# Shared expert's weights split into halves by the Pool engine during the last attention

## What is computed

```python
x = x + xattn(layernorm(x), ctx)     # 16 heads of 32; rms-normed q and k; image and text softmax apart, then summed
x = x + ffn(layernorm(x))            # 32 experts, 4 of them per token, capacity 80, and a shared expert

def ffn_shared(x):                   # shared_gate, shared_up, shared_down: 512x512 each
    return silu(x @ shared_gate.T) * (x @ shared_up.T) @ shared_down.T
```

## Time and profile before

| | |
|---|---|
| median of 3 runs | 1188.79 us (1188.22 to 1189.98) |
| the profiled execution's own time | 1194.59 us |
| its span | 1192.8 us |
| PE busy | 1116.2 us, 94% |
| DVE busy | 856.9 us, 72% |
| ACT busy | 650.6 us, 55% |
| POOL busy | 202.1 us, 17% |

### The profile page before, as it was taken

One profiled execution on the slowest core, in us unless ns is written; L12 is line 12 of the kernel. 1 busy time (PEld: TensorE's weight loads), 2 busy tenths in 40 slices (PEclk: granted clock), 3 DMA queues, 4 the chain that ended last, 5 costly groups with the idle time before them and its releaser, 6 DMA issues. The chain is left out here.

```text
span 1192.8 us, 21823 instructions
## 1 busy us (share of the span) xinstructions
PE 1116.2 (94%) x8948; PEld 415.7 (35%) x8948; DVE 856.9 (72%) x1056; ACT 650.6 (55%) x916; POOL 202.1 (17%) x307
## 2 busy tenths in 40 slices
PE   7899999999999989999999999887999989999996
PEld 3342223344222334322233432222544433333332
DVE  6777889897898988788889879997789842222221
ACT  5559997444999644699955469883311121221121
POOL 1220000243000024300002430002100021333442
PEclk9999999999999999999999999999999999999999
DMA  8851000768200096900028780104813337999742
GB/s 299 199 109 43 2 2 10 194 135 201 54 2 2 20 228 136 203 8 2 2 72 194 171 215 31 36 3 136 359 60 109 113 113 285 348 317 313 215 62 33
DMA packets 142860, 150.15 MB, mean 126 GB/s; under 512 B 108833, under 2 KB 109089, under 8 KB 137761
## 3 DMA queue, kind: packets, MB, share of 16 engines
q1 hardware_dynamic: 135328, 131.57, 38.1%
q0 software_dynamic: 5120, 10.82, 4.9%
q10 hardware_dynamic: 2304, 6.29, 2.2%
HBM read 101.96 MB, written 21.51 MB: 104 GB/s over the span
## 5 line engine op out<-in xcount | busy, mean ns | idle before, releaser
L718 ACT ACTIVATE work<-ps 128x1024 f32<-128x1024 f32 x384 | 372.3, 1022 | 30.7 <-PE ps L1215 15.0
L1221 PE MATMUL ps<-work,vals 128*32 128x512 f32 (+2 forms) x1664 | 220.3, 600 | 3.8 <-DVE nums L963 2.1
L1072 PE MATMUL ps<-wts,work 128*128 128x512 f16 x864 | 194.9, 379 | 11.1 <-DVE work L777 10.7
L1215 PE MATMUL ps<-quer,keys 32*128 32x512 f16 x2496 | 171.9, 377 | 22.2 <-ACT work L718 14.9
L975 DVE TENSOR_TENSOR work<-work 128x2048 f32<-128x2048 f32 x64 | 146.6, 2291 | 6.2 <-ACT work L718 0.5
L975 DVE TENSOR_TENSOR attn<-attn,work 128x2048 f32<-128x2048 f32 x62 | 142.0, 2290 | 5.4 <-ACT work L718 0.5
L1072 PEld LDWEIGHTS ps<-wts,work 128*128 128x128 f16 x864 | 83.3, 98 | 118.7 <-issue 19.3
L2040 PE MATMUL ps<-wring,xgt 128*80 128x512 f32 x256 | 114.9, 592 | 0.0
L1866 DVE COPY xgt<-ps 128x320 f32<-128x320 f32 x32 | 15.7, 491 | 137.8 <-PE ps L2031 137.8
L1072 PE MATMUL ps<-wts,hl 128*128 128x512 f16 x432 | 101.1, 386 | 12.0 <-DVE wts L759 7.3
L533 POOL TENSOR_SCALAR small<-small 128x1 f32<-128x1 f32 x68 | 20.5, 301 | 534.9 <-ACT work L628 534.9
(11 more groups left out here) (221 smaller groups left out, 1402.5 us busy)
## 6 DMA issues: line engine op xcount, KB each, us to landing
wring<-in_wx SPq DMA_DIRECT2D x32, 1536.0 KB, 9.1
raw<-in_ctx SPq DMA_DIRECT2D x52, 256.0 KB, 3.3
rb<-sums_inverse ACTq DMA_DIRECT2D x48, 128.0 KB, 3.8
work<-in_x SPq DMA_DIRECT2D x8, 512.0 KB, 4.8
table<-nums SPq DMA_DIRECT2D x16, 256.0 KB, 2.5
work<-in_x SPq DMA_DIRECT2D x12, 256.0 KB, 3.5
x<-work SPq DMA_DIRECT2D x12, 256.0 KB, 2.6
x2t_rows<-nums SPq DMA_DIRECT2D x12, 256.0 KB, 2.5
```

The source lines that it names most:

```text
L718: act.activation(prob[0:rows, s % PROBS, 2 * half:2 * half + 2, :], ps[0:rows, 2 * pair:2 * pair + 2, :], ACT.Exp, scale=SCALE, bias=pad i ...
L1072: mm = pe.matmul(out, lhs(a, c)[:, cols], wts[:, w, z, c * D:(c + 1) * D], start=(k == 0), stop=(k == len(steps) - 1))
L1215: mm = pe.matmul(ps[:, 2 * pair + h % 2, :], k[h * HD:(h + 1) * HD, :], q[h * HD:(h + 1) * HD, :], start=(e == 0), stop=(e == len(terms) - 1))
L1221: return pe.matmul(ps[h * HD:(h + 1) * HD, NUM, :], vals[a:z, ORDER[n], g * P + h * HD:g * P + (h + 1) * HD], prob[a:z, s % PROBS, h, :], ...
```

## The change

DVE's `ffn_weight` and its two calls go. Pool gets a `ffn_weight` of three instructions, called for the three weights in a row behind the filling of `sel`: it scales the f32 values by 256 where they lie, copies them to the high half as f16, and subtracts that from them into the low half. Between them it waits for its own semaphore. `f_wlo` is raised by the third.

```diff
@@ block.gpsimd
+            def ffn_weight(p, i):
+                pool.wait_ge(s_fw[i], 16 * (2 * p + 2 if i == 0 else p + 1))
+                own(pool.tensor_scalar(sstage[i][:, :], sstage[i][:, :], WS, None, ALU.mult))
+                own(pool.tensor_copy(swt[i][:, 0, :], sstage[i][:, :]))
+                pool.tensor_tensor(swt[i][:, 1, :], sstage[i][:, :], swt[i][:, 0, :], ALU.subtract).then_inc(f_wlo, 1)
+
             def one_pass(p):
...
                 ins.then_inc(s_const, 1)
+                for i in range(3):
+                    ffn_weight(p, i)
                 pool.wait_ge(s_xr, 16 * (2 * p + 2))
                 pool.wait_ge(a_den, gn(bb, NG - 1))
@@ block.vector
-            def ffn_weight(p, i):
-                dve.wait_ge(s_fw[i], 16 * (2 * p + 2 if i == 0 else p + 1))
-                dve.wait_ge(d_link, own(dve.tensor_scalar(swt[i][:, 0, :], sstage[i][:, :], WS, None, ALU.mult)))
-                dve.scalar_tensor_tensor(swt[i][:, 1, :], sstage[i][:, :], WS, swt[i][:, 0, :], ALU.mult,
-                                         ALU.subtract).then_inc(f_wlo, 1)
...
                     if bb < B:
                         image_sum(bb, g)
-                    elif b == B - 1 and g > 0:
-                        ffn_weight(p, g - 1)
...
                     dve.tensor_copy(nums[:, g, 1, :], ps[:, NUM, :]).then_inc(a_ni, 1)
-                    if bb == B - 1 and g > 0:
-                        ffn_weight(p, g - 1)
```

## The result

The changed kernel takes 1206.91 us (median of 4 runs, 1205.62 to 1208.71) against 1188.51 of the kernel before on the same chip. The ratio is 1.0142, 95% interval 1.0123 to 1.0161, so 18.4 us or 1.4% slower. The range held it; 1204.2 was forecast.

What follows compares the result with a forecast made beforehand. DVE was taken to bound the last batch's attention groups that split a weight, PE the others. A loss of 20.1 us less a gain of 4.7 gave +15.4 on 1188.8, so 1204.2 us, range 1197 to 1214.

Steps and rivals of the forecast that it cites:

- What bounds the stage, and the gain: Last batch's attention: DVE sets the pace in groups splitting a weight, otherwise PE; dropping DVE's split gains 4.7 us.
- The mechanism: From 715.7 to about 763, DVE's denominator adds and nine Pool instructions alternate; adds beside them take 4 to 7 us.
- Pool's price: Nine Pool instructions splitting three weights take 26.1 us in sum, bounds 24.9 and 33.3.
- by the iota: Pool's one-input operations over 2048 columns priced from the 2560-column iota at 1.04 ns per column: 2.1 us each.
- How much of it DVE stands still for: A DVE instruction with two SBUF operands stands still as long as a Pool instruction runs; 20.1 us lost.
- What is hidden: Of Pool's 26.1 us, 6.0 cost DVE nothing: add gaps 0.8, PSUM copies and idle time 3.1, slack 2.1.
- Pool's instructions hide (1): DVE held for only part of each Pool instruction, or Pool falls back; 1184.1 us, turning at 41%; chance 0.10.
- Dearer one-input operations (2): Pool's one-input operations cost more than the iota: 7.2 us more (1211.4) or 16.2 more (1220.4); chance 0.10.
- The clock (3): PE's clock falls to half in the stops of the new stretch: 6.5 us more, 1210.7; chance 0.08.

Runs made afterwards that it cites:

- experiment 2: The changed kernel with its nine Pool instructions replaced by nine memsets of the same sizes, written and not read; ratio 0.9970 to the kernel before.
- experiment 3: The changed kernel with Pool's three weights spread out, one in each group after the first; ratio 1.0158 to the kernel before.
- experiment 7: The changed kernel without the scaling in place, so Pool has two instructions per weight; ratio 1.0101 to the kernel before.
- experiment 11: The changed kernel without the scaling, TensorE's scores from step 8 repeated three times, step 15's six times, filling up to step 16; ratio 1.0098 to the kernel before.
- experiment 8: The changed kernel with TensorE computing the scores of steps 8 to 16 of the last batch three times over; ratio 1.0139 to the kernel before.

## Why the prediction was right, and where not

**What bounds the stage, and the gain: right.** Without DVE's split groups 1 and 2 fell by 2.16 and 2.07 us (2.23 and 2.14 were forecast) and group 3 by 0.57 (0.3): 4.8 for 4.7.

**The mechanism: right in the main.** Nine Pool instructions from 717.0 to 762.6 (715.7 to 763 was forecast), in turn with the adds, which took 3.8 to 6.0 us (4 to 7). ACT waited 19.6 us for them. Group 0 took 45.9, group 1 30.3, group 2 27.0 (45, 29, 27). That an add is held by what Pool reads, and not by Pool's being there, the rows ahead of the change couldn't tell; experiment 2 did.

**Pool's price: the term was mis-sized.** The sum of nine was put at 26.1 us with bounds 24.9 and 33.3; alone they take 34.0, over the upper one. The step that failed is the price of a one-input operation "by the iota": the cast took 1.89 for 2.1, but the scaling 5.4, and the estimate by the Trainium skill's 1.03 cycles (GPSIMD Engine Reference, section 3.1, Elementwise — side-by-side cycle accounting), 1.8 us, fits the cast and not the scaling. The subtraction took 4.06 for 4.49.

**How much of it DVE stands still for: a second term wrong, and luck.** The prediction had DVE stand still for as long as a Pool instruction runs. What I had taken for one thing are two: how long Pool works, and how long DVE is held. The scaling holds an add for 3.3 of its 5.4 us, the cast for 1.5 of 1.89, the subtraction for 3.7 of 4.06. Where an add meets each of the nine that makes 3 x 8.43 = 25.3 (25.1 in experiment 3), and the prediction's 26.1 less the gaps was 25.3 too. That the two agree is luck: the nine take 34.0 us alone, 7.9 more than forecast, and DVE is held for 8.7 less than these 34.0.

**What is hidden: a term that was too large.** From these 25.3 I took 3.1 us off for the copies and the idle time ahead of them, and 2.1 for slack, 5.2 in all. Of the first the change shows 25.3 - 23.1 = 2.2, in the third weight. Of the second it shows 23.1 - 22.2 = 0.9, or about 1.7 with the clock's 0.8 added back. The idle time of 0.7 ahead of the results copy stood in both of my terms, the wait ahead of the image copy stays in every plain group of experiment 3, and slack is 0.9 us a group and no more. So the loss was 25.3 - 2.2 - 0.9 = 22.2 for 20.1, and the net 17.4 in the stage for 15.4.

**Rivals.** Pool's instructions hide (1): its condition, that DVE is held for a part of each only, is true of the scaling, but DVE is held for 25.3 of Pool's 34.0 us, 74%, far over the 41% from which it would have turned. Dearer one-input operations (2): true of the scaling, by more than I gave it, and not of the cast; it came without the price, since what counts is the time held. The clock (3): it did fall, to 0.50 from 733 on, and I had given that 8%. But its price was 0.8 us in the change, not 6.5, because DVE set the pace meanwhile. It cost at least 2.3 us in experiment 7, where Pool was done before the clock had come back.

**What stays open.** The medians differ by 18.4 us, the stages by 17.4; 1.0 us is less than the scatter of the runs, and I don't assign it. Why the scaling takes near three times a cast, and at which point of it Pool lets DVE go on, isn't shown. Nor is the share of 0.9 us in experiment 11's group 1 that the added scores made.

## What to carry to other kernels

Work that is moved to an idle Pool isn't free if it reads SBUF while VectorE runs instructions with two SBUF operands: count the time for which those are held, not Pool's, and count it nearly in full where VectorE has little slack (here 0.9 us in a group of 27). Spreading it out doesn't help when each stretch is as tight as the next, and a wait that recurs in every round isn't slack. What did fit for free, in groups 1 and 2, were pieces small enough for the gaps of the two engines that had some (1024 columns on ScalarE and VectorE per group). The whole split in such pieces cost 108.1 - 105.9 = 2.2 us, against 4.8 on VectorE alone and 22.2 on Pool.

## What the runs showed of the hardware that I hadn't expected

- Pool, 128x2048, alone: memset 1.80 us, cast f32 to f16 1.89, subtraction with f16 result 4.06, scaling by a constant 5.37 to 5.40, whether to f32 or f16.
- Nine memsets on Pool left VectorE's two-operand adds at 2.29 us; one that reads held them for 1.5 (cast), 3.3 (scaling) and 3.7 us (subtraction).
- With TensorE busy for 3.8 of the 8 us from 725 to 733, and a stop of 4.0 us that ended at 734.8, its granted clock was 0.50 from 733 to 749; in experiment 8, with it busy for 7.6, 6.3 and 5.3 us of the three times 8 from 723 to 747, it stayed at 1.00.
